# A two-stage conditional residual kernel: first unit of x in three parts, convolution matrices loaded once and copied, the constants' product moved, unit 1 turned in two

## The chip, the cores and the metric

The kernel runs on one core of a Trainium2 chip. The metric is the device time in microseconds of one execution; the median of three runs is given. TensorE (PE) does the matrix products, VectorE (DVE), ScalarE (ACT) and GpSimd (POOL) the elementwise work, and SyncE (SP) and ScalarE each issue DMAs into a queue of their own; 16 DMA engines serve both queues.

## The reference, cut to what matters

Everything is float32. x is 128 samples x 64 channels x 1024 positions.

```python
def L0(x, c, weight, c_weight, bias):      # grouped convolution: 4 groups of 16 channels, 9 taps
    out = conv(x, weight, padding=4, groups=4)
    return out + (c @ c_weight.T)[:, :, None] + bias[None, :, None]

def L1(x, emb, W0, b0, W1, b1, W2, b2, weight, bias_k):
    h = gelu(emb @ W0 + b0); h = gelu(h @ W1 + b1)
    att = softmax(h @ W2 + b2)             # 8 experts for each sample
    agg_w = einsum('bk,koi->boi', att, weight[..., 0])
    agg_b = att @ bias_k
    return einsum('boi,bih->boh', agg_w, x) + agg_b[:, :, None]

x = x + L0(x, cond_128, L0_cond_weight, L0_cond_c_weight, fside_S_0)
x = x + L1(x, cond_128, ...)
```

So each sample gets a grouped convolution, then a 64 x 64 mixing matrix of its own. Both residual sums are folded into the matrices by adding an identity, and everything that does not depend on x is folded into one constant for each sample and output channel.

## The kernel before, in words

**Units.** The 128 samples are worked on in 16 units of 8. Two buffers `xin` and two `xph` are used in turn (the "slot"). For each unit:

1. Eight DMAs bring x into `xin`: halves `i` of the length (0 by SP's queue, 1 by ScalarE's), times `k` in 0, 1 and `t` in 0, 1 (`x_piece`). Partitions hold half, group and sample; each of the 16 partitions of a DMA receives 8 rows of 516 positions.
2. VectorE turns them (`turn_in`, L418) so that 4 neighbouring positions of 16 channels lie on partitions: `xin` to `xph`. The semaphore `turned` counts these turns.
3. TensorE convolves (`conv`, L552): four groups `g`, each 12 matmuls of 64 x 512, with the matrices `wsum` (a view of `wraw`, whose two partition halves hold the same numbers) into a pair of PSUM banks `yps`. Groups take the two pairs in turn, so group `g` waits until VectorE has emptied that of `g-2`.
4. VectorE transposes each group out of PSUM (`y_columns`, L444), and when all four are there it transposes them again into `ynat` (`y_natural`, L453).
5. TensorE mixes (`mix`, L575): four outputs `o` (two samples each), 4 matmuls each, from `ynat` and the unit's mixing matrices `mixv` into `zps`; output `o` waits until `zps` of `o-2` is empty.
6. ScalarE evacuates with the constant added (`evacuate`, L311), two activations an output, and makes `mixv` of the next unit (`matrices`, L320) from the table of all matrices, `mixt`.
7. SP stores each output.

TensorE's order is software-pipelined: conv of unit u, groups 0 and 1; mix of u-1, outputs 0 and 1; conv groups 2 and 3; mix outputs 2 and 3. A matmul is listed as two passes in the trace (float32), so 24 matmuls read x48. Every engine's order is that of its own program (`@block.tensor` and so on); semaphores alone tie them. Units 0 to 2 and the last ones are written out, the others are in loops of two units.

**The opening.** Before the first mix, the small network (`mm`, `act_mlp`, `soft`) gives `att`; GpSimd adds the identities; two aggregates of 16 matmuls each (`aggregate`, L533) produce all mixing matrices, and ScalarE gathers each in two pieces (`gather`, L324). The constants come from one product of `beta` with `consts` (`output_constants`, L651), ScalarE's copy (L359), sums on GpSimd (L275 to L282) and one more product (`pair_constants`, L657). `keep_on` are dummy matmuls on zeros. Unit 0's x comes in two parts and is turned in two (`first_phases`); unit 1's in one part, turned in one.

**ScalarE and SP issue loads in program order**, each load of unit u behind a wait for `turned`, and each instruction after it in the engine's program is behind that wait as well.

## Time and profile before

| | us |
|---|---|
| median of 3 runs | 252.69 |
| lowest, highest | 251.22, 255.4 |
| the profiled execution | 251.88 |
| its span in the profile | 250.1 |

The profiled execution is 1.78 us longer than its span; the difference lies around the span.

| engine | busy us | share of the span |
|---|---|---|
| TensorE | 238.8 | 96% |
| VectorE | 220.8 | 88% |
| ScalarE | 128.5 | 51% |
| GpSimd | 10.4 | 4% |

DMA queue 1 is SP's, queue 10 ScalarE's. In 68.6 MB of traffic the mean is 274 GB/s. Times in a timeline count from the start of the span. A row of it merges neighbouring instructions of one line; its first number is the start, the second the time to the end of the last, and in brackets stands how long the engine was idle before it and what ended that.

### The profile page before, as it was taken

Reading aid. Unit: us, or ns where it says so; the run is one execution under the profiler, and the core shown is the slowest. Engines: PE = TensorE matmul, PEld = TensorE weight load, DVE = VectorE, ACT = ScalarE, POOL = GpSimd, SP = SyncE. Lnnn points to the kernel's source line nnn. Section 1 sums busy time; section 2 is a strip of 40 time slices with the busy share of each in tenths; the row PEclk is TensorE's granted clock in tenths of the full one; section 3 lists DMA queues with packets and bytes.
Section 4 is the critical chain, followed back from the end, with each engine's and each line's share of the span. In section 5 each row is a group of like instructions: output and inputs, shape, how many; then the busy total and the mean of one; then the engine's idle time right before and its main releaser. Section 6 shows DMA issues by size and latency. Waiting matters only on the chain.

```text
span 250.1 us, 5822 instructions
## 1 busy us (share of the span) xinstructions
PE 238.8 (96%) x2186; PEld 103.0 (41%) x2186; DVE 220.8 (88%) x115; ACT 128.5 (51%) x208; POOL 10.4 (4%) x36
## 2 busy tenths in 40 slices
PE   7899899999999999999999999999999999999962
PEld 5633234444343444444443444344443444444631
DVE  0256699999999999999999999999999999999672
ACT  2564106534719083745639181836547286273863
POOL 1323200000000000000000000000000000000000
PEclk9799999999999999999999999999999999999999
DMA  7999935999989999999999998999989895444466
GB/s 201 260 290 273 270 66 184 263 317 369 362 300 303 334 242 375 240 387 233 358 264 313 317 301 310 258 381 229 377 241 348 271 313 242 168 170 169 168 246 260
DMA packets 29771, 68.60 MB, mean 274 GB/s; under 512 B 3312, under 2 KB 5744, under 8 KB 29760
## 3 DMA queue, kind: packets, MB, share of 16 engines
q1 hardware_dynamic: 19824, 51.12, 61.7%
q10 hardware_dynamic: 9936, 17.34, 26.2%
q8 instruction: 7, 0.11, 0.2%
q14 instruction: 4, 0.03, 0.0%
HBM read 34.89 MB, written 33.55 MB: 274 GB/s over the span
## 4 chain that ended last, share of the span: by engine, by line
PE 83%; DVE 5%; DMA 4%; ACT 3%; ACTq 2%; issue 1%
PE yps L552 59%; PE zps L575 21%; DMA xin<-in_x 4%; DVE xph L418 2%; DVE ynat L453 2%; PE yps L591 1%; ACTq L330 1%; PE yps L634 1%; DVE ycol L444 1%; ACT mixv L320 1%; ACT zout L311 1%; DVE ynat L498 1%; PE zps L614 0%; PE yps L614 0%; PE zps L603 0%
## 5 line engine op out<-in xcount | busy, mean ns | idle before, releaser
L552 PE MATMUL yps<-xph,wraw 64*64 64x512 f32 x1488 | 166.7, 589 | 1.7 <-DVE ycol L444 1.1
L552 PEld LDWEIGHTS yps<-xph,wraw 64*64 64x64 f32 x1488 | 66.5, 132 | 95.1 <-issue 95.0
L311 ACT ACTIVATE zout<-zps,gamu 128x512 f32<-128x512 f32 x120 | 72.8, 689 | 29.8 <-PE zps L575 19.9
L444 DVE STREAM_TRANSPOSE ycol<-yps 128x1024 f32<-128x1024 f32 x62 | 74.5, 1227 | 7.3 <-PE yps L552 5.5
L320 ACT ACTIVATE mixv<-mixt 64x256 f32 (+1 forms) x64 | 42.3, 660 | 67.0 <-issue 65.8
L418 DVE STREAM_TRANSPOSE xph<-xin 128x4160 f32<-128x4160 f32 (+2 forms) x17 | 71.8, 4223 | 3.9 <-DMA xin<-in_x 3.9
L453 DVE STREAM_TRANSPOSE ynat<-ycol 128x4096 f32<-128x4096 f32 x15 | 66.7, 4445 | 1.1
L575 PE MATMUL zps<-ynat,mixv 64*64 64x512 f32 x480 | 59.4, 592 | 0.4 <-DVE ynat L453 0.2
L575 PEld LDWEIGHTS zps<-ynat,mixv 64*64 64x64 f32 x480 | 20.6, 132 | 31.6 <-issue 31.2
L250 POOL COPY gamu<-gam 128x4 f32 (+1 forms) x16 | 2.9, 188 | 197.9 <-ACT zout L311 193.2
L634 PE MATMUL yps<-zout 128*128 128x256 f32 x26 | 9.8, 538 | 1.3 <-POOL zout L252 1.3
L634 PEld LDWEIGHTS yps<-zout 128*128 128x128 f32 x26 | 6.7, 271 | 3.3 <-POOL zout L252 1.3
L591 PE MATMUL yps<-xph,wraw 64*64 64x256 f32 x96 | 6.0, 375 | 0.0
L462 DVE TENSOR_REDUCE negmax<-zps 128x1 f32<-128x8 f32 x1 | 0.2, 167 | 6.4 <-PE zps L670 6.4
L491 DVE STREAM_TRANSPOSE ycol<-yps 128x256 f32<-128x256 f32 x8 | 3.1, 424 | 2.6 <-PE yps L591 2.6
L591 PEld LDWEIGHTS yps<-xph,wraw 64*64 64x64 f32 x96 | 4.4, 132 | 2.5 <-issue 1.6
L324 ACT ACTIVATE mixt<-zps 128x1024 f32<-128x1024 f32 x4 | 3.9, 1021 | 2.4 <-PE zps L533 2.4
L498 DVE STREAM_TRANSPOSE ynat<-ycol 128x1024 f32<-128x1024 f32 x4 | 4.7, 1224 | 0.1
L332 ACT ACT_TABLE_LOAD x1 | 1.3, 1283 | 3.8 <-issue 3.8
L603 PE MATMUL zps<-ynat,mixv 64*64 64x512 f32 x16 | 2.2, 600 | 1.0 <-ACT zout L311 1.0
L363 ACT ACTIVATE gam<-zps 128x64 f32<-128x64 f32 x1 | 0.2, 224 | 5.5 <-PE zps L657 5.5
L533 PE MATMUL zps<-zout 32*64 32x512 f32 x32 | 2.9, 612 | 0.0
(54 smaller groups left out, 30.2 us busy)
## 6 DMA issues: line engine op xcount, KB each, us to landing
out<-zout SPq DMA_DIRECT2D x60, 512.0 KB, 4.6
xin<-in_x ACTq DMA_DIRECT2D x60, 258.0 KB, 7.4
xin<-in_x SPq DMA_DIRECT2D x60, 258.0 KB, 7.1
out<-xin SPq DMA_DIRECT2D x2, 512.0 KB, 4.2
out<-xin SPq DMA_DIRECT2D x4, 256.0 KB, 2.8
xin<-in_x ACTq DMA_DIRECT2D x4, 132.0 KB, 5.3
xin<-in_x SPq DMA_DIRECT2D x4, 130.0 KB, 5.9
xin<-in_x SPq DMA_DIRECT2D x4, 128.0 KB, 7.5
```

Of the source, the lines that this page charges most:

```text
L311: nc.scalar.activation(zout[:, o].rearrange("p (i c j q) -> p c i j q", i=2, c=2, q=PH)[:, c], zps[:, at:at + BANK].rearrange("p (q i j) - ...
L320: nc.scalar.activation(mix_places(slot, h, d), mix_values(u, d), ACT.Copy).then_inc(mixv_made, 1)
L324: nc.scalar.activation(mixt[:, a, 2 * RO * i:2 * RO * i + 2 * RO].rearrange("p c b -> p (c b)"), zps[:, 2 * BANK * i:2 * BANK * i + 2 * BA ...
L418: nc.vector.transpose(xph[slot][:, :, :, at:to].rearrange("q g s j t -> q j s g t"), xin[slot][:, :, PH * at:PH * to].rearrange("q c (j p) ...
L444: nc.vector.transpose(ycol[:, :, :, :, :, g].rearrange("p i s j q c -> p (i s j) q c"), yps[:, 2 * BANK * (g % 2):2 * BANK * (g % 2) + 2 * ...
L453: nc.vector.transpose(ynat[slot][:].rearrange("p t q i s (j l) -> p (i s j) q t l", l=16), ycol[:].rearrange("p i s j q g c -> p (i s j q ...
L491: nc.vector.transpose(ycol[:, i, 2 * sh:2 * sh + 2, :, :, g].rearrange("p s j q c -> p (s j) q c"), y_last(g)[:, i].rearrange("p (n j t) - ...
L498: nc.vector.transpose(ynat[1][:, :, :, i, 2 * sh:2 * sh + 2].rearrange("p t q s (j l) -> p (s j) q t l", l=16), ycol[:, i, 2 * sh:2 * sh + ...
L552: last = nc.tensor.matmul(yps[C * c:C * c + C, at:at + BANK].rearrange("p (s f) -> p s f", s=S // 2), wsum[rows, b, g], xph[slot][rows, g, ...
L575: last = nc.tensor.matmul(zps[C * s:C * s + C, at:at + BANK].rearrange("p (n j) -> p n j", j=NJ), mixv[slot][rows, 2 * o + s], ynat[slot][ ...
L591: last = nc.tensor.matmul(y_last(g)[C * c:C * c + C, i].rearrange("p (s f) -> p s f", s=2), wsum[rows, b, g], xph[1][rows, g, 2 * sh:2 * s ...
L634: nc.tensor.matmul(yps[:, 3 * BANK:3 * BANK + BANK // 2], still[:, 0:P], still[:, 0:BANK // 2], start=True, stop=True)
```

## The change

- Unit 0's x comes in three parts instead of two, cut at columns 60 and 95 of 130 (`CUTS`; a column is 4 positions), and is turned in three. A DMA row of 264 to 252 positions becomes rows of 236 or 240, 140, and 140 or 136. ScalarE's 12 x issues of unit 0 are spread between its small steps.
- The convolution matrices, the same on both partition halves, are loaded for 64 partitions; a VectorE copy makes the other 64.
- The mixing weights are issued by ScalarE, not SP; SP issues `consts` ahead of the last part of x.
- An activation on a single column (`spare`) stands right behind the second gelu, so that the exp table's load does.
- The first aggregate goes to `yps` and the second to `zps`, so they no longer wait for each other's gathers; the constants' product goes to a bank of `yps` (`cps`), ahead of the first convolution, with one `keep_on` behind it.
- Unit 1's x is turned in two pieces, before the column transposes of groups 1 and 2 of unit 0.
- `matrices` stands ahead of `load` in ScalarE's program, in the written-out units and in the loop.

```diff
+CUTS = 0, 60, 95, 2 * NJ + 2
+        cps = yps[:, 2 * BANK:3 * BANK]
...
-            sp.dma_start(mixw, mix_w).then_inc(mix_in, 16)
-            for part, there in ((0, x_first), (1, x_in[0])):
+            for part in range(3):
+                if part == 2:
+                    sp.dma_start(consts, const_w).then_inc(const_in, 16)
                 for k in range(KQ):
                     for t in range(2):
-                        sp.dma_start(*x_piece(0, 0, 0, k, t, part)).then_inc(there, 16)
-            sp.dma_start(consts, const_w).then_inc(const_in, 16)
+                        sp.dma_start(*x_piece(0, 0, 0, k, t, part)).then_inc(x_part[part], 16)
...
-                act.wait_ge(turned, u)
+                act.wait_ge(turned, 3 if isinstance(u, int) and u == 2 else u + 2)
...
-            act.dma_start(wraw[:], conv_w).then_inc(w_in, 16)
...
+            def first_load(part, k):
+                for t in range(2):
+                    act.dma_start(*x_piece(0, 0, 1, k, t, part)).then_inc(x_part[part], 16)
+
+            act.dma_start(wraw[0:C], conv_w).then_inc(w_in, 16)
+            act.dma_start(mixw, mix_w).then_inc(mix_in, 16)
+            first_load(0, 0)
+            first_load(0, 1)
...
+            nc.scalar.activation(spare[:], still[:, 0:1], ACT.Exp)
...
+            load_block(1, 1, 0)
+            gather(0, 1, 4)
+            gather(0, 0, 8)
+            act.wait_ge(const_mm, 1)
+            nc.scalar.activation(gprod.rearrange("p e c -> p (e c)"), cps, ACT.Copy).then_inc(const_out, 1)
             load_block(1, 1, 1)
...
                         if o == 1:
+                            matrices(2 * i + c - 3, 1 - c)
                             load(2 * i + c, c)
-                            matrices(2 * i + c - 3, 1 - c)
...
+            def second_phases(c):
+
+                if c == 0:
+                    dve.wait_ge(x_in[1], 128)
+                turn_in(1, (NJ + 2) * c, NJ + 2 + NJ * c)
...
+            dve.wait_ge(w_in, 16)
+            nc.vector.tensor_copy(wraw[C:P], wraw[0:C]).then_inc(w_both, 1)
...
-            first_aggregate()
-            keep_on(3)
-            second_aggregate()
-            pe.wait_ge(w_in, 16)
+            aggregates()
+            output_constants()
+            keep_on(1)
             pe.wait_ge(w_sum, 1)
+
+            pe.wait_ge(agg_out, 2)
             conv(0, 0, 0)
-            conv(0, 0, 1, (output_constants,))
+
+            pe.wait_ge(const_out, 1)
+            conv(0, 0, 1)
```

**ScalarE, units 1 and 2** (L311/L315 evacuates, L294/L298 issues loads of x, L320/L324 makes matrices). Before:

```order
L294 DMA xin<-in_x 16x8x516 x4
L311 ACTIVATE zout<-zps,gamu 128x2x256 x4
L294 DMA xin<-in_x 16x8x516 x4
L320 ACTIVATE mixv<-mixt 64x16x16 x4
L311 ACTIVATE zout<-zps,gamu 128x2x256 x4
```

And changed:

```order
L298 DMA xin<-in_x 16x8x516 x4
L315 ACTIVATE zout<-zps,gamu 128x2x256 x4
L324 ACTIVATE mixv<-mixt 64x16x16 x4
L298 DMA xin<-in_x 16x8x516 x4
L315 ACTIVATE zout<-zps,gamu 128x2x256 x4
```

The four matrices passed ahead of the four issues of the loads; the loop has the same two orders.

**VectorE, from the network's maximum to the natural transpose of unit 0.** Before:

```order
L462 TENSOR_REDUCE negmax<-zps 128x1
L464 RECIPROCAL erec<-esum 128x1
L418 STREAM_TRANSPOSE xph<-xin 128x66x4x4x2
L418 STREAM_TRANSPOSE xph<-xin 128x64x4x4x2
L444 STREAM_TRANSPOSE ycol<-yps 128x128x8
L418 STREAM_TRANSPOSE xph<-xin 128x130x4x4x2
L444 STREAM_TRANSPOSE ycol<-yps 128x128x8 x3
L453 STREAM_TRANSPOSE ynat<-ycol 128x32x4x2x16
```

And changed, from the new copy on:

```order
L475 COPY wraw<-wraw 64x832
L477 TENSOR_REDUCE negmax<-zps 128x1
L479 RECIPROCAL erec<-esum 128x1
L428 STREAM_TRANSPOSE xph<-xin 128x60x4x4x2
L428 STREAM_TRANSPOSE xph<-xin 128x35x4x4x2 x2
L456 STREAM_TRANSPOSE ycol<-yps 128x128x8
L428 STREAM_TRANSPOSE xph<-xin 128x66x4x4x2
L456 STREAM_TRANSPOSE ycol<-yps 128x128x8
L428 STREAM_TRANSPOSE xph<-xin 128x64x4x4x2
L456 STREAM_TRANSPOSE ycol<-yps 128x128x8 x2
L465 STREAM_TRANSPOSE ynat<-ycol 128x32x4x2x16
```

Unit 0's two turns became three, and the one turn of unit 1 (128x130) became two (66 and 64 columns) around the column transpose of group 1.

**TensorE, from the softmax's transpose to the first convolutions.** Before:

```order
L674 MATMUL zps<-shares,att 128x128
L634 MATMUL yps<-zout 128x256 x3
L533 MATMUL zps<-zout 64x512 x8
L634 MATMUL yps<-zout 128x256 x3
L533 MATMUL zps<-zout 64x512 x8
L552 MATMUL yps<-xph,wraw 64x512 x16
L651 MATMUL zps<-zout,beta 128x512
L552 MATMUL yps<-xph,wraw 64x512 x32
```

And changed:

```order
L686 MATMUL zps<-shares,att 128x128
L648 MATMUL yps<-zout 128x256 x3
L547 MATMUL yps<-zout 64x512 x8
L547 MATMUL zps<-zout 64x512 x8
L663 MATMUL yps<-zout,beta 128x512
L648 MATMUL yps<-zout 128x256
L566 MATMUL yps<-xph,wraw 64x512 x48
```

The dummies between the aggregates went, and the constants' product moved from the second group of convolutions to ahead of the first.

## Rows read from the trace of the kernel before

**Rows 1.** The page: busy us (share of the span) xinstructions.

```profile
PE 238.8 (96%) x2186; PEld 103.0 (41%) x2186; DVE 220.8 (88%) x115; ACT 128.5 (51%) x208; POOL 10.4 (4%) x36
```

**Rows 2.** Timeline of TensorE in the loop: start us, us, what.

```profile
38.19 5.37 PE L552 MATMUL yps<-xph,wraw 64*64 64x512 f32 x48
...
51.93 5.37 PE L552 MATMUL yps<-xph,wraw 64*64 64x512 f32 x48
57.09 1.93 PE L575 MATMUL zps<-ynat,mixv 64*64 64x512 f32 x16
58.81 5.37 PE L552 MATMUL yps<-xph,wraw 64*64 64x512 f32 x48
63.97 2.17 PE L575 MATMUL zps<-ynat,mixv 64*64 64x512 f32 x16
65.92 5.37 PE L552 MATMUL yps<-xph,wraw 64*64 64x512 f32 x48
...
225.22 5.37 PE L552 MATMUL yps<-xph,wraw 64*64 64x512 f32 x48
```

**Rows 3.** Timeline of ScalarE in the loop (ACTq is its DMA issuing).

```profile
56.83 2.85 ACTq L294 DMA_DIRECT2D xin<-in_x  x4
59.73 2.72 ACT L320 ACTIVATE mixv<-mixt 64x256 f32<-64x256 f32 x4 [5.92 <-issue]
62.48 2.42 ACT L311 ACTIVATE zout<-zps,gamu 128x512 f32<-128x512 f32 x4
```

**Rows 4.** Timeline of VectorE in the loop, one period apart.

```profile
50.03 2.38 DVE L444 STREAM_TRANSPOSE ycol<-yps 128x1024 f32<-128x1024 f32 x2
...
63.65 2.38 DVE L444 STREAM_TRANSPOSE ycol<-yps 128x1024 f32<-128x1024 f32 x2
```

**Rows 5.** Timeline of VectorE in the opening.

```profile
7.91 0.17 DVE L462 TENSOR_REDUCE negmax<-zps 128x1 f32<-128x8 f32 x1 [6.45 <-PE zps L670]
...
14.86 2.31 DVE L418 STREAM_TRANSPOSE xph<-xin 128x2048 f32<-128x2048 f32 x1 [1.51 <-DMA xin<-in_x]
...
21.91 4.51 DVE L418 STREAM_TRANSPOSE xph<-xin 128x4160 f32<-128x4160 f32 x1 [0.37 <-DMA xin<-in_x]
...
30.57 1.25 DVE L444 STREAM_TRANSPOSE ycol<-yps 128x1024 f32<-128x1024 f32 x1 [1.88 <-PE yps L552]
31.86 4.45 DVE L453 STREAM_TRANSPOSE ynat<-ycol 128x4096 f32<-128x4096 f32 x1
```

**Rows 6.** Timeline of TensorE in the opening.

```profile
12.50 1.11 PE L533 MATMUL zps<-zout 32*64 32x512 f32 x16
...
15.03 1.77 PE L533 MATMUL zps<-zout 32*64 32x512 f32 x16
17.43 3.67 PE L552 MATMUL yps<-xph,wraw 64*64 64x512 f32 x32 [0.62 <-DVE xph L418]
21.02 1.12 PE L651 MATMUL zps<-zout,beta 80*128 80x512 f32 x2
22.08 4.53 PE L552 MATMUL yps<-xph,wraw 64*64 64x512 f32 x40
27.70 2.81 PE L552 MATMUL yps<-xph,wraw 64*64 64x512 f32 x24 [1.09 <-DVE ycol L444]
...
36.45 1.95 PE L575 MATMUL zps<-ynat,mixv 64*64 64x512 f32 x16 [0.25 <-DVE ynat L453]
```

**Rows 7.** Timeline of ScalarE in the opening.

```profile
5.39 1.25 ACTq L339 DMA_DIRECT2D xin<-in_x  x2
```

**Rows 8.** Timeline of GpSimd in the opening.

```profile
15.80 1.27 POOL L270 TENSOR_TENSOR zout<-zout,shares 64x512 f32<-64x512 f32 x1 [4.76 <-DMA zout<-in_const_w]
```

**Rows 9.** DMA traffic of two stretches, 4 to 12 us and 16 to 20 us.

```profile
DMA packets 2314, 2.13 MB, mean 266 GB/s; under 512 B 264, under 2 KB 2299, under 8 KB 2314
...
DMA packets 725, 1.35 MB, mean 337 GB/s; under 512 B 73, under 2 KB 73, under 8 KB 725
```

**Rows 10.** Stretches: us, busy (xcount) PE, PEld, DVE, ACT, POOL; granted clock; DMA share; GB/s.

```profile
6.00:7.00 1.00, 0.29 (x2) 0.09 (x1) 0.00 (x0) 0.31 (x1) 0.00 (x0) 1.00 1.12 294
9.00:10.00 1.00, 1.00 (x4) 0.72 (x3) 0.00 (x0) 0.00 (x0) 0.97 (x4) 0.50 1.11 251
```

More of the change, by code:

```diff
@@ L76, in build @@
         ones = sb("ones", [1, P])
-        warm = sb("warm", [P, 1])
+        warm, spare = sb("warm", [P, 1]), sb("spare", [P, 1])
         negmax, esum, erec = sb("negmax", [P, 1]), sb("esum", [P, 1]), sb("erec", [P, 1])
@@ L145, in build @@
         x_from, x_to = (0, H - PAD), (H + PAD, L)
-        x_cut = [i * H + Q + PAD for i in range(2)]
         def x_piece(slot, u, i, k, t, part=None):
-            at, to = ((x_from[i], x_to[i]) if part is None else
-                      ((x_from[i], x_cut[i]), (x_cut[i], x_to[i]))[part])
+            at, to = x_from[i], x_to[i]
+            if part is not None:
+                at = max(at, H * i + PH * CUTS[part] - PAD)
+                to = min(to, H * i + PH * CUTS[part + 1] - PAD)
             return x_places(slot, i, k, t, at, to - at), x_block(u, k, t, at, to - at)
@@ L193, in load @@
                 if not (isinstance(u, int) and u < 2):
-                    sp.wait_ge(turned, u)
+                    sp.wait_ge(turned, 3 if isinstance(u, int) and u == 2 else u + 2)
                 for k in range(KQ):
@@ L337, in _ @@
             nc.scalar.activation(h1, sps[:, 0:NS], ACT.Gelu, bias=b0s).then_inc(act_mlp, 1)
-            for t in range(2):
-                act.dma_start(*x_piece(0, 0, 1, 1, t, 1)).then_inc(x_in[0], 16)
+            first_load(1, 1)
             act.wait_ge(mm, 2)
             nc.scalar.activation(h2, sps[:, NS:2 * NS], ACT.Gelu, bias=b1s).then_inc(act_mlp, 1)
+            nc.scalar.activation(spare[:], still[:, 0:1], ACT.Exp)
+            first_load(2, 0)
             act.wait_ge(soft, 1)
@@ L365, in _ @@
                 evacuate(0, 0, o)
+                if o == 1:
+                    matrices(1, 1)
                 if o % 2 == 1:
                     load(3 + o // 2, 1 - o // 2)
-                if o == 1:
-                    matrices(1, 1)
             for o in range(PR):
@@ L372, in _ @@
                 if o == 1:
+                    matrices(2, 0)
                     load(5, 1)
-                    matrices(2, 0)
             with act.Fori(3, NU // 2) as i:
@@ L387, in _ @@
             act.wait_ge(gam_cut, NU)
-            act.wait_ge(turned, NU)
+            act.wait_ge(turned, NU + 2)
             def evacuate_first(o, c):
@@ L464, in _ @@
             nc.vector.reciprocal(erec[:], esum[:]).then_inc(soft, 1)
-            first_phases(0)
-            first_phases(1)
+            for part in range(3):
+                first_phases(part)
             y_columns(0, 0)
-            phases(1, 1)
+            second_phases(0)
             y_columns(0, 1)
+            second_phases(1)
             y_columns(0, 2)
@@ L527, in aggregate @@
             def aggregate(a):
-                for r in range(RT):
-                    if a > 0 and r % 2 == 0:
-                        pe.wait_ge(agg_out, 2 * a - 1 + r // 2)
+                for r in ((2, 3, 0, 1), range(RT))[a]:
                     for d in range(2):
-                        nc.tensor.matmul(zps[C * d:C * d + C, BANK * r:BANK * r + BANK],
+                        nc.tensor.matmul((yps, zps)[a][C * d:C * d + C, BANK * r:BANK * r + BANK],
                                          mixw[32 * r:32 * r + 32, 2 * a + d],
@@ L541, in conv @@
                 if g == 0:
-                    pe.wait_ge(turned, u + 2)
+                    pe.wait_ge(turned, 3 if isinstance(u, int) and u == 0 else u + 4)
                 if not (isinstance(u, int) and u < 1 and g < 2):
@@ L649, in output_constants, with pair_constants @@
                 pe.wait_ge(const_eye, 1)
+                pe.wait_ge(agg_out, 1)
+                nc.tensor.matmul(cps, beta[:], consts, start=True, stop=True).then_inc(const_mm, 1)
+            def pair_constants():
                 pe.wait_ge(agg_out, CH)
-                nc.tensor.matmul(gps, beta[:], consts, start=True, stop=True).then_inc(const_mm, 1)
-            def pair_constants():
-                pe.wait_ge(const_out, 1)
                 pe.wait_ge(const_sum, 6)
```

50 lines of the change are left out of this document (19 added, 31 removed).

## The prediction, as it stood before the changed kernel was run

> **What bounds the kernel now.** I read the page's busy shares first: TensorE is busy in 96% of the span and VectorE in 88% [rows 1]. So the span is one stream of matmuls, plus whatever delays its start or breaks it. I then read TensorE's timeline for breaks. After the opening it is regular: 48 convolution passes and 16 mixing passes, start to start 6.88 us (51.93 to 58.81 [rows 2]). From the start at 38.19 to that at 225.22 there are 27 such periods, 187.03 us, where 27 x 6.88 would be 185.6. So about 1.4 us of breaks lie in the loop, and they are not spread evenly: one period of 7.11 us (58.81 to 65.92) is typical of six of them, and each has its excess inside the mixing passes (2.17 us at 63.97 instead of 1.93 at 57.09).
>
> ScalarE's timeline at the same place names the cause [rows 3]. It issues the next unit's four loads in 2.85 us, from 56.83, once VectorE has turned the unit before; only then does it make the mixing matrices (59.73, 2.72 us), and only then evacuate outputs 2 and 3 (62.48 to 64.90). The second mix of TensorE's next pair needs both of those PSUM halves free, and it starts right behind 64.90. ScalarE is half idle and yet late, because its work stands behind an issue that waits. VectorE is the next bound: its own shortest period is 13.62 us [rows 4], against 2 x 6.88 = 13.75 of TensorE.
>
> In the opening, three things end waits [rows 5, 6]. Unit 0's x lands in two parts; VectorE turns the second at 14.86 to 17.17, and the first convolution starts at 17.43, after 0.62 us in which TensorE had nothing to do. Unit 1's x lands at 21.9; it is turned in one piece of 4.51 us, and the column transpose that TensorE needs for group 3 stands behind it, so TensorE idles 1.09 us until 27.70. Then VectorE waits 1.88 us for that group, and starts the natural-order transpose of unit 0 at 31.86; the first mix starts 0.14 us behind its end [rows 6]. From 31.86 both streams run closely packed, so **the time at which this transpose starts (31.86) is what the opening is worth**, one to one.
>
> **The loop.** ScalarE now makes the matrices ahead of the loads. They need only an earlier evacuation and the gathered weights, so they fit in the idle 5.92 us that stands ahead of them now [rows 3]. The loads keep their time, because they wait for the same turned unit in both kernels (the count is raised by two only because units 0 and 1 count two more turns), and four short activations can stand queued while ScalarE's sequencer issues. The evacuation of outputs 2 and 3 follows the issue directly, near 59.8 instead of 62.48, over 2 us before TensorE needs it. **This takes the whole 1.4 us**; VectorE's 13.62 leaves it free, barely. The other end is 0, if some other wait sits in the same place. I take 1.4, since the end of the evacuation and the resumption of the mix coincide.
>
> **The opening on the engines.** ScalarE has one issue more ahead of its first table load (the mixing weights, about 0.4 us). The two matmuls of the small network and its exp shift by about that much; two x issues take 1.25 us [rows 7], and four more of them stand between ScalarE's small steps, each where it waits anyway. The new copy of the convolution matrices on VectorE (64 x 832) is bounded by the 1.25 us column transpose of 1024 elements above [rows 5] and nothing below; it runs in the 6.45 us in which VectorE waits for the network [rows 5], so it costs nothing. Behind it waits only GpSimd's sum on these matrices, which has several us to spare. The aggregates start at 12.50 and 15.03 now, with a gather and dummies between them [rows 6]. Now they stand back to back: twice the 1.11 us of the first, and 0.4 for the delay, end near 15.1. The constants' product needs GpSimd's sum of 1.27 us, which starts at 15.80 today, when its load lands [rows 8]. The load moves ahead of the last x part, so 408 KB less stand before it on SP's queue (mixing weights 128, x 280). At half of 266 GB/s [rows 9] that is 3.1 us: a sum from 13 to 14.3, before TensorE asks. Then the product (1.06, from 21.02 to the next pass at 22.08 in the trace of now) and one dummy of 0.4: TensorE is ready at 16.6, and carries no product between convolutions any more.
>
> **The opening on the DMA queues.** Here the change works against itself. It saves 208 KB of matrices, but x of unit 0, 2048 packets of about 1 KB, becomes 1024 packets of 944 to 960 bytes and 2048 of 544 to 560. The prices: from 4 to 12 us, 2314 packets and 2.13 MB in 8 us, that is 3.46 ns a packet of 920 bytes on average; from 16 to 20 us, 725 packets and 1.35 MB in 4 us, 5.52 ns a packet of 1862 [rows 9]. A straight line through both gives 1.45 ns per packet plus bytes at 457 GB/s. The cut adds 1024 packets and 128 completion packets (16 for each of 8 more DMAs): 1152 x 1.45 ns = +1.7 us. The matrices save 0.21 MB and 64 packets: -0.55 us. Net +1.15 us before unit 1's x is complete. Bounds: by bytes alone the cut is free (net -0.47 us); by packets alone, 1152 x 3.46 ns = +4.0 less 0.2. I take the line, as it uses both rows; 560 bytes lie outside them.
>
> The last part of unit 0 then lands at 14.86 + 1.15 + 0.5 (the constants' load is now ahead of it) less up to 1.2 for traffic of unit 1 that today is served before it and will now be issued after: about 15.7 (13.8 to 17). Its turn is 35 columns of the 64 that take 2.31 us, 1.27 us, so **the first convolution starts near 17.2**, later than TensorE's 16.6. Four groups (twice 5.37), then a column transpose and handovers, 1.4: the natural transpose can start at 17.2 + 12.1 = 29.3.
>
> Unit 1's x lands at 21.9 + 1.15 = 23.0. Two of its eight transfers are now issued by ScalarE behind the constants' copy, near 16 instead of near 11, but the queue ahead of them is hardly empty by then. After it: half a turn 2.38, column 1.2, half a turn 2.31, two columns 2.4: 23.0 + 8.3 = **31.3**. This is the later of the two, so the opening brings 31.86 - 31.3 = 0.55 us. TensorE's 1.09 us stall goes (group 3 needs the column at 26.7), yet VectorE, with unit 1's x, is late next, and takes most of it back.
>
> Sum: 1.4 + 0.55 = 2.0 us off the profiled execution of 251.88 us (span 250.1): 249.9. That execution lies 0.8 below the median of the runs shown, 252.69, whose three values are 4 us apart; I go half of that way and forecast **250.3**.
>
> The Trainium skill, *DMA: Bandwidth & Descriptors*, Specifications, asks for transfers of at least 512 bytes for line rate; pieces of 560 bytes pass, so by it the cut would be free and the sum that of rival A. The rows speak against it: 920-byte packets moved 266 GB/s and 1862-byte ones 337.
>
> **The rivals.**
> (A) *Bytes are all that count.* Unit 1's x lands at 21.9 - 0.5 = 21.4, the last part of unit 0 at 13.8, and TensorE's 16.6 decides the start. The transpose starts at max(16.6 + 12.1, 21.4 + 8.3) = 29.7, or at 28.7 if unit 2's loads press less. Gain 2.2 to 3.2, with the loop 3.6 to 4.6; 251.88 - 4.1 + 0.4 = 248.2. For it: both rows of the line are averages over mixed traffic, and neither measures 560 bytes. Against: the two rates [rows 9]. Chance 0.20. The rule of that page, worked out here, is this case.
> (B) *Packets are all that count*: slower than before. Unit 1's x lands at 21.9 + 3.8 = 25.7, the transpose starts at 34.0, 2.1 late; with the loop's 1.4 the kernel is 0.7 slower: 253.0. It decides as soon as the cut delays unit 1's x by over 3.1 us in all. For it: 560 bytes lie outside both rows, and a fixed cost can rule there. Against: packets of twice the size took 1.6 times as long. Chance 0.10.
> (C) *The loop's breaks stay*, because ScalarE cannot run the matrices beside the issue, or VectorE takes over: only the opening, 251.7. Chance 0.15.
> (D) *The clock.* TensorE was 0.29 busy at 6 to 7 us, and its granted clock was 0.50, the lower of its two levels, at 9 to 10 [rows 10]. A dummy block between aggregates is gone, and about 0.6 us may be idle before the first convolution, or more if x is late. Should some 3 us of the first convolutions run at that level, they would cost 1.6 us more; with a start at 17.2 that gives 30.9, just under the 31.3 of unit 1's x, so it shows only where that x is early or the dip is longer: 250.8. Chance 0.08.
> My forecast, with the opening between -0.3 and +1.3: 0.47.
>
> **How the numbers follow.** The range must reach A and C and most of the scatter of a median; B lies beyond it: 247.7 to 252.6. A measurement here tells about 2% (5 us) from no change. Only the best of A with luck in the runs passes 247.6: 0.08. No case reaches 257.7: 0.02. Within 2%: 0.90.
>
> **What would show it.** Right: all mixing blocks in the loop at 1.93 us; ScalarE's matrices starting before its load issues; the last part of x(0) turned by 17; unit 1's first half turned from 23.0; the natural transpose at 31.3. If the first half turn begins by 21.5, A holds; after 25, B. Mixing blocks of 2.1 us and more mean C; a granted clock of 0.5 past 15 us means D. The forecast is wrong if the natural transpose starts outside 30.5 to 32.2, or if a new wait appears at the constants' product.

## The result, and the profile after

The changed kernel takes **255.75 us** (median of 6 runs, 254.19 to 259.19), the kernel before 252.3 in the same comparison: ratio 1.015, 95% interval 1.0116 to 1.0184. It is slower by 1.5%, where 250.3 was forecast with a range of 247.7 to 252.6; it stays within 2% of the kernel before, as was forecast with 0.90. Ratios leave out the slow runs of a kernel, those more than 1.5% above its fastest, and medians are of all its runs.

The profiled execution took 257.73 us, with a span of 255.9: 5.8 us more than the 250.1 before, and 2 us above its own median, so it shows the loss larger than it mostly is.

The loop first. TensorE's timeline (start us, us, what), answering to [rows 2]:

```profile
52.11 5.37 PE L566 MATMUL yps<-xph,wraw 64*64 64x512 f32 x48
...
58.98 5.37 PE L566 MATMUL yps<-xph,wraw 64*64 64x512 f32 x48
64.14 1.93 PE L589 MATMUL zps<-ynat,mixv 64*64 64x512 f32 x16
65.86 5.37 PE L566 MATMUL yps<-xph,wraw 64*64 64x512 f32 x48
...
231.08 5.37 PE L566 MATMUL yps<-xph,wraw 64*64 64x512 f32 x48
```

and ScalarE's, answering to [rows 3]:

```profile
60.75 2.74 ACT L324 ACTIVATE mixv<-mixt 64x256 f32<-64x256 f32 x4
64.18 2.81 ACTq L298 DMA_DIRECT2D xin<-in_x  x4
67.10 2.42 ACT L315 ACTIVATE zout<-zps,gamu 128x512 f32<-128x512 f32 x4 [3.61 <-PE zps L589]
```

The matrices are made before the issue, and the evacuation starts at 67.10, directly behind the end of the issue (64.18 + 2.81 = 66.99) and about 1 us behind the mix that it empties (64.14 + 1.93); before, it started 3.5 us behind its mix. The profile puts ScalarE's 3.61 us of waiting down to TensorE, but both outputs were computed by 66.07; what it waited for last was its own issue. From 52.11 to 231.08 there are 26 periods of 6.883 us on average, against 6.927 before: the mixing blocks of over 2 us are gone, 1.2 us over the loop. That step did what it was forecast to do.

The opening is where the time went. VectorE, answering to [rows 5]:

```profile
9.56 3.40 DVE L428 STREAM_TRANSPOSE xph<-xin 128x1920 f32<-128x1920 f32 x2
14.75 1.35 DVE L428 STREAM_TRANSPOSE xph<-xin 128x1120 f32<-128x1120 f32 x1 [1.78 <-DMA xin<-in_x]
20.08 1.25 DVE L456 STREAM_TRANSPOSE ycol<-yps 128x1024 f32<-128x1024 f32 x1 [3.98 <-PE yps L566]
29.17 2.38 DVE L428 STREAM_TRANSPOSE xph<-xin 128x2112 f32<-128x2112 f32 x1 [7.84 <-DMA xin<-in_x]
...
37.62 1.25 DVE L456 STREAM_TRANSPOSE ycol<-yps 128x1024 f32<-128x1024 f32 x1 [1.62 <-PE yps L566]
38.91 4.45 DVE L465 STREAM_TRANSPOSE ynat<-ycol 128x4096 f32<-128x4096 f32 x1
```

and TensorE, answering to [rows 6]:

```profile
15.74 1.10 PE L663 MATMUL yps<-zout,beta 80*128 80x512 f32 x2 [0.43 <-ACT mixt L329]
...
17.20 7.97 PE L566 MATMUL yps<-xph,wraw 64*64 64x512 f32 x72
32.82 4.74 PE L566 MATMUL yps<-xph,wraw 64*64 64x512 f32 x24 [7.66 <-DVE ycol L456]
```

The first turn of unit 1's x, which waits for all of it, starts at 29.17 instead of 21.91, 7.26 us later. The two-piece turn gave 2.14 back (group 3 starts at 32.82, 5.12 later than 27.70). Group 3 then took 4.74 us instead of 2.81. The stretches of the same trace (us; busy of PE, PEld, DVE, ACT, POOL; granted clock; DMA share; GB/s) tell why:

```profile
29.00:30.00 1.00, 0.00 (x0) 0.00 (x0) 0.83 (x1) 0.00 (x0) 0.00 (x0) 0.97 1.08 198
33.00:34.00 1.00, 1.00 (x8) 0.40 (x11) 1.00 (x1) 0.00 (x0) 0.00 (x0) 0.50 0.00 0
```

TensorE had idled since 25.2, and its granted clock stood at 0.50, the lower level, from 30 to past 36. So 7.26 - 2.14 + 1.93 = 7.05 us, which is the natural transpose at 38.91 instead of 31.86; less 1.2 of the loop, 5.85, the span's 5.8.

Why was x late? DMA traffic from 14 to 22 us, of before (first group of lines) and of after (second); q1 is SP's queue, q10 ScalarE's; packets, MB, share of 16 engines:

```profile
DMA packets 1326, 2.43 MB, mean 303 GB/s; under 512 B 151, under 2 KB 151, under 8 KB 1326
q1 hardware_dynamic: 735, 1.34, 59.0%
q10 hardware_dynamic: 591, 1.09, 47.0%
```

```profile
DMA packets 1042, 1.92 MB, mean 240 GB/s; under 512 B 112, under 2 KB 112, under 8 KB 1042
q1 hardware_dynamic: 754, 1.39, 79.2%
q10 hardware_dynamic: 288, 0.53, 28.2%
```

The shares of both queues add up to over 100% in either kernel, so the engines had packets at hand. SP's queue moved as much as before, ScalarE's half as much. ScalarE's issues, in the timeline of its queue, and SP's of unit 2 (duration min/median/max in ns, first and last start):

```profile
11.46 0.60 ACTq L298 DMA_DIRECT2D xin<-in_x  x1
12.09 0.62 ACTq L298 DMA_DIRECT2D xin<-in_x  x1
...
16.88 1.39 ACTq L298 DMA_DIRECT2D xin<-in_x  x2
18.37 1.24 ACTq L298 DMA_DIRECT2D xin<-in_x  x2
```

```profile
L202 SPq DMA_DIRECT2D xin<-in_x x4: 577/600/601, 16.1 to 18.0; - x4
```

The first block of unit 1 goes out at 11.46 and the second at 16.88, behind the constants' copy, where the kernel before had 8.1 and 10.9. SP's four of unit 1 go out from 10.23 instead of 8.25, so all eight are later, not two. By 16.88 SP has begun with unit 2.

### The profile page after: what moved, and what is told of

Same layout as the page of the kernel before. It is cut to its first block, busy times and chain, and to the rows that moved or that the text cites. A ratio compares the mean times of both kernels' runs of the same rounds, so it can differ in the third digit from the quotient of the medians.

```text
span 255.9 us, 5835 instructions
## 1 busy us (share of the span) xinstructions
PE 238.2 (93%) x2182; PEld 105.0 (41%) x2182; DVE 220.8 (86%) x118; ACT 127.2 (50%) x209; POOL 10.4 (4%) x36
## 4 chain that ended last, share of the span: by engine, by line
PE 83%; DMA 5%; DVE 4%; ACT 3%; ACTq 2%; issue 1%
PE yps L566 58%; PE zps L589 20%; DMA xin<-in_x 5%; DVE ynat L465 2%; PE yps L648 2%; ACTq L334 2%; PE yps L605 1%; DVE ycol L456 1%; DVE xph L428 1%; ACT mixv L324 1%; ACT zout L315 1%; DVE ynat L514 0%; PE yps L547 0%; PE zps L628 0%; PE yps L663 0%
## 5 line engine op out<-in xcount | busy, mean ns | idle before, releaser
L566 PE MATMUL yps<-xph,wraw 64*64 64x512 f32 x1488 | 168.4, 595 | 7.7 <-DVE ycol L456 7.7
L315 ACT ACTIVATE zout<-zps,gamu 128x512 f32<-128x512 f32 x120 | 72.8, 689 | 95.7 <-PE zps L589 76.3
L566 PEld LDWEIGHTS yps<-xph,wraw 64*64 64x64 f32 x1488 | 67.8, 134 | 100.9 <-issue 100.8
L428 DVE STREAM_TRANSPOSE xph<-xin 128x4160 f32<-128x4160 f32 (+4 forms) x19 | 72.0, 3795 | 9.8 <-DMA xin<-in_x 9.8
L589 PE MATMUL zps<-ynat,mixv 64*64 64x512 f32 x480 | 58.3, 589 | 0.3 <-DVE ynat L465 0.3
L324 ACT ACTIVATE mixv<-mixt 64x256 f32 (+1 forms) x64 | 42.4, 663 | 1.9 <-ACT mixt L329 0.7
L589 PEld LDWEIGHTS zps<-ynat,mixv 64*64 64x64 f32 x480 | 21.9, 133 | 29.1 <-issue 28.7
L648 PE MATMUL yps<-zout 128*128 128x256 f32 x22 | 8.7, 552 | 1.3 <-POOL zout L256 1.3
L648 PEld LDWEIGHTS yps<-zout 128*128 128x128 f32 x22 | 5.8, 279 | 2.8 <-POOL zout L256 1.3
L605 PEld LDWEIGHTS yps<-xph,wraw 64*64 64x64 f32 x96 | 4.4, 132 | 2.5 <-issue 1.6
L475 DVE COPY wraw<-wraw 64x832 f32<-64x832 f32 x1 | 0.6, 586 | 3.3 <-DMA wraw<-in_conv_w 3.3
L617 PE MATMUL zps<-ynat,mixv 64*64 64x512 f32 x16 | 2.2, 600 | 1.0 <-ACT zout L315 1.0
L329 ACT ACTIVATE mixt<-yps 128x1024 f32<-128x1024 f32 x2 | 1.9, 1020 | 2.1 <-PE yps L547 2.1
```

What stands on the lines that cost most here:

```text
L315: nc.scalar.activation(zout[:, o].rearrange("p (i c j q) -> p c i j q", i=2, c=2, q=PH)[:, c], zps[:, at:at + BANK].rearrange("p (q i j) - ...
L324: nc.scalar.activation(mix_places(slot, h, d), mix_values(u, d), ACT.Copy).then_inc(mixv_made, 1)
L428: nc.vector.transpose(xph[slot][:, :, :, at:to].rearrange("q g s j t -> q j s g t"), xin[slot][:, :, PH * at:PH * to].rearrange("q c (j p) ...
L566: last = nc.tensor.matmul(yps[C * c:C * c + C, at:at + BANK].rearrange("p (s f) -> p s f", s=S // 2), wsum[rows, b, g], xph[slot][rows, g, ...
L589: last = nc.tensor.matmul(zps[C * s:C * s + C, at:at + BANK].rearrange("p (n j) -> p n j", j=NJ), mixv[slot][rows, 2 * o + s], ynat[slot][ ...
L605: last = nc.tensor.matmul(y_last(g)[C * c:C * c + C, i].rearrange("p (s f) -> p s f", s=2), wsum[rows, b, g], xph[1][rows, g, 2 * sh:2 * s ...
```

## Experiments

**1. The late block, three ways.** Theory L: the late issue alone. *issue_early*, on the changed kernel:

```diff
             load_block(1, 1, 0)
+            load_block(1, 1, 1)
             gather(0, 1, 4)
...
-            load_block(1, 1, 1)
             gather(1, 0, 12)
```

> The changed kernel, with ScalarE's second block of unit 1's x (two transfers of 258 KB) issued right behind its first block again, ahead of the gathers, near 12.7 to 14 us instead of 16.9 to 18.3. Theory L (late issue: the block stands behind the constants' copy and so falls behind unit 2's loads on the DMA engines): unit 1's x is complete by 21 to 22.5 instead of 29.2, TensorE's 7.7 us of waiting for group 3 goes, the natural transpose of unit 0 starts at 29.5 to 31 instead of 38.9, and the kernel takes 247.5 to 250 where the one before takes 252.3. Rival P (the smaller packets and more transfers of unit 0 are what delays unit 1's x): the block's place changes little, unit 1's x still lands after 26, time 253 to 255.5. Rival S (unit 2's loads, which SP issues 1.1 us earlier than in the kernel before, take the engines in any case): lands at 24 to 26, time 250.5 to 252.5.

Measured: 254.06 us (251.6 to 255.69), ratio 1.006 (1.0033 to 1.0087), 0.9% better than the changed kernel's 1.015. Unit 1's x still came late (in the slowest of the twelve runs, 255.69):

```profile
27.98 2.38 DVE L428 STREAM_TRANSPOSE xph<-xin 128x2112 f32<-128x2112 f32 x1 [5.43 <-DMA xin<-in_x]
```

Theory L in this simple form fell: issuing at 12.4 to 15.0 does not do. P's numbers (after 26, 253 to 255.5) were met, so this run alone does not refute P; *late_on_before* and *cut_only* below do. What the trace shows instead is a queue alone. From 16 to 18 us SP's had the engines to itself, at under 200 GB/s:

```profile
DMA packets 221, 0.39 MB, mean 197 GB/s; under 512 B 30, under 2 KB 30, under 8 KB 221
q1 hardware_dynamic: 221, 0.39, 107.2%
```

*sp_hold*, on the changed kernel:

```diff
-                    sp.wait_ge(turned, 3 if isinstance(u, int) and u == 2 else u + 2)
+                    sp.wait_ge(turned, 4 if isinstance(u, int) and u == 2 else u + 2)
```

> The changed kernel, with SP's loads of unit 2 held until the first half of unit 1 has been turned (count 4 instead of 3); ScalarE's late second block of unit 1 stays at 16.9. Theory L with unit 2 as the competitor: without SP's traffic after 16 us the two late transfers have the engines almost alone, land 4 to 6 us after their issue, so unit 1's x is complete at 22 to 24, and the kernel takes 249.5 to 251.5. Rival P: lands at 27 or later, time above 254. Rival Q (one queue alone gets only the 200 to 220 GB/s that the trace shows where the other is idle, and is slow whoever competes): lands at 24 to 26, time 251.5 to 253.5.

Measured: 253.84 us, ratio 1.0088 (1.0066 to 1.0111), 0.6% better than the changed kernel:

```profile
25.78 2.38 DVE L428 STREAM_TRANSPOSE xph<-xin 128x2112 f32<-128x2112 f32 x1 [4.66 <-DMA xin<-in_x]
```

The landing is in rival Q's range, the time 0.3 us above it. Without unit 2's traffic 3.4 of the 7.26 us go and the rest stays. ScalarE's queue, alone from 24 to 28 us, moved 199 GB/s, so the late queue is slow when nothing competes too.

*late_on_before*, on the kernel before:

```diff
-            load_block(1, 1, 1)
             gather(0, 0)
...
             gather(1, 1)
+            load_block(1, 1, 1)
```

> The kernel before, with one edit: ScalarE's second block of unit 1's x issued behind the four gathers, near 17 us instead of 10.9. Theory L: the loss appears without any other part of the change; unit 1's x lands at 26 to 29 instead of 21.9, the natural transpose of unit 0 starts 4 to 7 us later, time 256.5 to 259.5. Rival P: the kernel before keeps its larger pieces, so it loses under 1.5 us, time 252.3 to 254. Rival S: within 1 us as well.

Measured: 255.67, 261.28, 262.11 and 262.46 us, too few and too far apart for a ratio. Even the lowest is 3.8 us above the median of the kernel before (251.83), without any other part of the change. P and S, which allowed up to 254 and up to 1 us, are out. L's range began at 256.5; why the other three runs lose about 10 us is open. In the run of 261.28:

```profile
30.05 4.51 DVE L418 STREAM_TRANSPOSE xph<-xin 128x4160 f32<-128x4160 f32 x1 [6.89 <-DMA xin<-in_x]
```

**2. The matrices ahead of the loads, alone.** *swap_on_before*: `matrices` ahead of `load` at the three places, as in the change.

> The kernel before, with the mixing matrices ahead of the loads in ScalarE's program and nothing else. My step on the loop: the six long mixing blocks go, 1.4 us less, ratio 0.993 to 0.996, time 250.6 to 251.3. Rival: they depend on how the two streams happen to lie after the opening and come back elsewhere, ratio 0.999 to 1.001.

Measured: 250.57 us, ratio 0.9954 (0.9934 to 0.9974), 1.3 us below the kernel before (251.83 in that comparison). Every full mixing block of its loop takes 1.92 or 1.93 us, so the step on the loop is shown by itself.

**3. Which part of the pairing counts.** Theory H now: each half of the partitions takes some 200 GB/s, SP fills one and ScalarE the other, and whoever issues late leaves a half idle. *halves_mixed*, on the changed kernel (SP likewise, `x_piece(slot, u, i, 0, t)`):

```diff
-            def load_block(u, slot, k):
-                for t in range(2):
-                    act.dma_start(*x_piece(slot, u, 1, k, t)).then_inc(x_in[slot], 16)
+            def load_block(u, slot, t):
+                for i in (1, 0):
+                    act.dma_start(*x_piece(slot, u, i, 1, t)).then_inc(x_in[slot], 16)
```

> The changed kernel, with the eight transfers of a unit (units 1 to 15) dealt out otherwise: SP issues k=0 of both halves of the length by turns, ScalarE k=1 of both by turns; before, SP wrote only partitions 0 to 63 and ScalarE only 64 to 127. Places and times of issue stay. Theory H (the two queues are served in about the order of issue, so after a late issue one queue runs alone, and alone it moves 200 GB/s because it writes one half of the partitions; both halves together take 335 to 340): the stretches at 200 GB/s between 14 and 30 us go up to 300 or more, unit 1's x is complete at 22 to 25 instead of 29.2, time 249.5 to 252. Rival R (a queue alone gets 200 GB/s whatever it writes): rates stay, lands at 28 to 30, time 253.5 to 256. The Trainium skill, SBUF - State Buffer, section Door 1, says that DMA bandwidth depends on how many of 16 ports the partitions reach, and partitions 64 and up use the other eight; by it H.

Measured: 258.82 us, ratio 1.0272 (1.0222 to 1.0322), unit 1's turn at 31.00: worse than both theory H (249.5 to 252) and rival R (253.5 to 256). The rates stayed, as R says: 204 to 245 GB/s in every 2 us from 14 to 30. The same edit on *swap_on_before*, *mixed_on_swap*:

> The kernel before with the matrices ahead of the loads, and the transfers of units 1 to 15 dealt out so that each queue writes both halves of the partitions by turns. Theory H: the stretches with one queue alone (12 to 14, 20 to 24, 28 to 32 us at 195 to 235 GB/s) get faster, unit 1's x lands up to 1 us earlier than 21.7, time 249.5 to 250.5; the loop gains nothing, its loads land 10 us ahead of need. Rival R: no change from the swap alone, 250.6. It can lose, landing at 22 to 24, if both queues now often write the same half at once.

Measured: 253.73 us, ratio 1.0052 (1.0016 to 1.0087), 1% above the swap alone in ratio (0.9954), unit 1's turn at 23.31. Here both queues work side by side from 16 to 20 us, and yet:

```profile
DMA packets 582, 1.07 MB, mean 267 GB/s; under 512 B 65, under 2 KB 65, under 8 KB 582
```

where the kernel before moved 337 in the same stretch [rows 9]. My expectation that a lone queue would speed up was wrong. It fits that its transfers are worked through one after the other, each in one half, and that two busy queues whose halves sometimes coincide lose; neither run shows which half a packet went to.

*port_bench* tests the halves by themselves, with loads behind the last store of the kernel before:

> The kernel before, with four stretches of loads after its last store, one after the other (the results are not touched; the time is longer by them and not compared): (1) SP alone, 8 transfers of 258 KB into partitions 0 to 63; (2) SP alone, 4 transfers of 512 KB into all 128 partitions; (3) SP into partitions 0 to 63 and ScalarE into 64 to 127, 4 transfers each at the same time; (4) both queues into 0 to 63. If the halves set the rate: about 200, 300 or more, 335, 200 GB/s. If the number of queues sets it: 200, 200, 335, 335. If the size of a row does: (2) alone rises, (1) and (3) alike.

DMA traffic inside the four stretches, in their order:

```profile
DMA packets 865, 1.59 MB, mean 199 GB/s; under 512 B 95, under 2 KB 95, under 8 KB 865
...
DMA packets 439, 1.61 MB, mean 402 GB/s; under 512 B 46, under 2 KB 46, under 8 KB 439
...
DMA packets 955, 1.78 MB, mean 254 GB/s; under 512 B 95, under 2 KB 95, under 8 KB 955
q1 hardware_dynamic: 488, 0.91, 53.3%
q10 hardware_dynamic: 467, 0.87, 52.2%
...
DMA packets 753, 1.39 MB, mean 199 GB/s; under 512 B 78, under 2 KB 78, under 8 KB 753
q1 hardware_dynamic: 399, 0.74, 56.7%
q10 hardware_dynamic: 354, 0.66, 50.6%
```

One queue into partitions 0 to 63: 199 GB/s. One queue into all 128: 402 (its rows are of 4 KB, not 2, and one transfer covers all partitions, not 16). Two queues into the same half: 199 again. So the number of queues does not set the 200; where they write does. That it is the half is not separated from the narrower reading: in the fourth stretch both queues issue their transfers for the same 16 partitions in the same order, and no run sent 4 KB rows into one half. Two queues into both halves, started together, gave 254 and not 335. The rate per us shows them taking turns: from 274 to 275 us SP's queue moved 97 packets and ScalarE's 26, in the next 22 and 104, at 231 GB/s both times. The Trainium skill, SBUF - State Buffer, section Door 1, has DMA bandwidth depend on how many of 16 ports the partitions reach, eight of them for partitions 0 to 63; by that, the trace agrees (199 and 402).

*paired_issue*, on the changed kernel:

```diff
             first_load(2, 1)
+            load_block(1, 1, 0)
             act.wait_ge(share_in, 16)
...
-            load_block(1, 1, 0)
+            load_block(1, 1, 1)
             gather(0, 1, 4)
...
-            load_block(1, 1, 1)
             gather(1, 0, 12)
```

> The changed kernel, with ScalarE's two blocks of unit 1's x where the kernel before has them: the first ahead of the four scaled attention copies (near 10.5), the second right behind these (near 12), so that they stand beside SP's four at 10.2 to 12.9. Theory H: both halves are written at the same time, 330 GB/s from 14.5 on, unit 1's x complete at 20.5 to 22; TensorE waits under 1 us for group 3; natural transpose of unit 0 at 29 to 30.5; time 248 to 249.5, under both kernels. Rival P (small packets): lands after 24, time over 251. If only lateness counted and not the pairing, this would equal the run with both blocks behind the copies (254.1).

Measured: 250.57 us (248.9 to 253.16), ratio 0.9956 (0.9918 to 0.9994): 1.9% (5 us) less than the changed kernel by moving four issues, two by about 1 us and two by 5. Above the 248 to 249.5 expected, but with all other parts of the change in place. In its profile, the fastest run:

```profile
22.44 2.38 DVE L428 STREAM_TRANSPOSE xph<-xin 128x2112 f32<-128x2112 f32 x1 [1.34 <-DMA xin<-in_x]
...
30.44 4.45 DVE L465 STREAM_TRANSPOSE ynat<-ycol 128x4096 f32<-128x4096 f32 x1
```

The 330 GB/s that I expected from 14.5 us on came only from 19 us on. From 14 to 18 both queues worked, each into its own half, and moved little more than one alone:

```profile
DMA packets 489, 0.90 MB, mean 226 GB/s; under 512 B 51, under 2 KB 51, under 8 KB 489
q10 hardware_dynamic: 262, 0.50, 59.0%
q1 hardware_dynamic: 227, 0.40, 48.8%
```

So pairing the issues makes the high rate possible and does not ensure it. What it does bring here is that ScalarE's transfers are no longer served behind SP's of unit 2.

*sp_takes_block*: ScalarE's late `load_block(1, 1, 1)` goes, and in SP's program

```diff
             load(1, 1)
+            for t in range(2):
+                sp.dma_start(*x_piece(1, 1, 1, 1, t)).then_inc(x_in[1], 16)
             load(2, 0)
```

> The changed kernel, with the two late transfers of unit 1's x (258 KB each, partitions 96 to 127) issued by SP right behind its own four, near 12.9 to 14.1 us, and no longer by ScalarE at 16.9. Theory O (the queues are served in about the order of issue, whatever queue it is; the loss comes from two transfers issued behind unit 2's): unit 1's x complete at 21.5 to 24, time 249.5 to 252.5. Rival (it is ScalarE's queue that is slow, in itself): no difference to see between this and an early issue by ScalarE, whose run took 251.6 to 255.7. If the smaller pieces were the cause, it stays at 255.

Measured: 253.19 us, ratio 1.0056 (0.9999 to 1.0113), unit 1's turn at 24.51, both just outside theory O's ranges. The landing is 3.5 us before that of *issue_early*, but the time is the same (ratio 1.006), which is what the rival had said; the run decides nothing by its time. That ScalarE's queue is not slow in itself rests on the rates of a queue alone: SP's 197 GB/s (*issue_early*, 16 to 18 us), ScalarE's 199 (*sp_hold*, 24 to 28).

**4. The other parts.** *two_turns*, on *swap_on_before*: `second_phases` as in the change, and the counts of `turned`.

> The kernel before with the matrices ahead of the loads and unit 1 turned in two pieces around the column transpose of group 1; x, weights and product as before. My formula: the natural transpose of unit 0 starts at the landing of unit 1's x (21.7) + 8.3 = 30.0 instead of 31.7, TensorE's 1.06 us wait goes, so 1.5 us less than the run with the swap alone (250.6): 249.1, ratio to before 0.987 to 0.991. Rival: the column that group 3 needs is only 2.2 us earlier while the natural transpose waits for the same end of the convolutions, gain under 0.5 us.

Measured: 248.92 us (248.33 to 249.36), ratio 0.9886 (0.9849 to 0.9922), 1.65 below the swap alone:

```profile
22.27 2.38 DVE L418 STREAM_TRANSPOSE xph<-xin 128x2112 f32<-128x2112 f32 x1 [0.23 <-DMA xin<-in_x]
...
31.04 4.45 DVE L457 STREAM_TRANSPOSE ynat<-ycol 128x4096 f32<-128x4096 f32 x1
```

That is 8.77 us from landing to natural transpose, where I had 8.3: in 0.58 of it VectorE waits for group 3.

*both_before*, on *two_turns*: `load_block(1, 1, 1)` directly behind `load_block(1, 1, 0)`, ahead of the attention copies.

> The run with two turns (248.92), with both of ScalarE's blocks of unit 1's x issued ahead of the attention copies, 8.5 to 11 us, beside SP's four at 8.3 to 10.9. If pairing the issue times is what keeps both halves of the partitions busy, unit 1's x is complete at 20.8 to 21.7 instead of 22.2 and the natural transpose of unit 0 starts 0.3 to 0.7 us earlier, 248.3 to 248.7. Rival: already paired enough, under 0.2 us, or the attention copies, now up to 0.5 us later, take it back.

Measured: 248.53 us, ratio 0.9858 (0.9827 to 0.9888); natural transpose at 30.36. That is 0.4 us less than *two_turns*, as expected, but the intervals overlap: a gain is not shown.

*old_loads*, on *paired_issue*:

```diff
-CUTS = 0, 60, 95, 2 * NJ + 2
+CUTS = 0, NJ + 2, 2 * NJ + 2
...
-            act.dma_start(wraw[0:C], conv_w).then_inc(w_in, 16)
-            act.dma_start(mixw, mix_w).then_inc(mix_in, 16)
+            act.dma_start(wraw[:], conv_w).then_inc(w_in, 16)
```

(`mixw` is issued by SP again, and the copy goes.)

> The run with the paired issue (250.57 median, 248.9 to 253.2), with the opening's loads as in the kernel before: unit 0's x in two parts, the convolution matrices loaded whole and not copied, mixing weights from SP; the constants' load ahead of the last part, the product ahead of the convolutions and unit 1 in two turns stay. If the three parts, the half load and the copy are what separates the paired run from the run with two turns alone (248.92), this gives 248.3 to 249.3, and little scatter. If it is the product and the aggregates' new place, it gives 250 to 251.5. The constants' load has 1 KB pieces ahead of it, so the product may wait 1 us.

Measured: **248.17 us** (248.03 to 248.97), ratio 0.985 (0.9818 to 0.9881): the fastest of all here. TensorE convolves all four groups in one stretch and VectorE does not wait for x:

```profile
18.24 10.54 PE L561 MATMUL yps<-xph,wraw 64*64 64x512 f32 x96
```

```profile
15.24 2.31 DVE L426 STREAM_TRANSPOSE xph<-xin 128x2048 f32<-128x2048 f32 x1 [1.24 <-DMA xin<-in_x]
...
22.30 2.34 DVE L426 STREAM_TRANSPOSE xph<-xin 128x2112 f32<-128x2112 f32 x1
```

*cut_only* and *half_weights* put back the three parts, or the half load with its copy and the mixing weights issued by ScalarE:

> The run old_loads (248.17: product ahead, unit 1 in two turns, matrices ahead of loads, transfers paired), with unit 0's x in three parts at 60 and 95 again, ScalarE's issues spread as in the changed kernel; weights whole, mixing weights by SP. If the three parts cost the 2.4 us (twelve issues instead of eight put ScalarE's transfers of unit 1's x two issues later, 10.5 to 13.2, so less paired with SP): 249.5 to 251, with scatter. If they cost nothing: 248 to 248.6. If my packet price (+1.7 us) were right, the landing of unit 0's last part would move to 16 or later; bytes alone leave it near 14.9.

> The run old_loads, with the convolution matrices loaded for 64 partitions and copied by VectorE, and the mixing weights issued by ScalarE; x in two parts. 208 KB less to load, at 200 to 340 GB/s 0.6 to 1 us, so unit 0's x lands that much earlier: 247.4 to 248.1. Rival: ScalarE's extra issue shifts its x transfers by 0.6 us against SP's and costs as much, 248.2 to 249.5.

Measured: 249.45 us, ratio 0.9923 (0.9896 to 0.9951), and 248.9, ratio 0.9885 (0.9853 to 0.9917). The three parts cost about 0.7% in ratio; of the half load no gain can be seen, where 247.4 to 248.1 was expected. *cut_only* also tests the packet price by itself. With it the last part of unit 0 would be turned from 16 or later. It was turned from 15.12, against 15.24 in *old_loads*:

```profile
15.12 1.35 DVE L428 STREAM_TRANSPOSE xph<-xin 128x1120 f32<-128x1120 f32 x1 [1.68 <-DMA xin<-in_x]
```

So the 1024 packets more did not delay it.

*late_on_old_loads*, on *old_loads*: ScalarE's two blocks of unit 1 where the changed kernel has them.

> The run old_loads, with ScalarE's first block of unit 1's x behind the attention copies and the second behind the constants' copy, as in the changed kernel; all other loads as in the kernel before. If the late issue is the whole cause of the loss, it takes 253.5 to 257 and unit 1's x lands at 26 to 30. If the loss needs the new parts as well, under 251.

Measured: ten runs from 250.48 to 257.83 us, median 255.3. Five of them, 250.48 to 253.75, give the ratio 1.0003 (0.996 to 1.0046), 1.5% or about 3.8 us above *old_loads*; the other five, 256.85 to 257.83, lie about 9 us above it, and why the times scatter so is open. In the profiled one (257.32), unit 1's x was turned from 28.47, in the range expected, and ScalarE's transfers issued at 12.49 and 13.11 got nothing from 14 to 18 us while SP's, issued from 8.35, were served:

```profile
DMA packets 440, 0.80 MB, mean 199 GB/s; under 512 B 48, under 2 KB 61, under 8 KB 440
q1 hardware_dynamic: 440, 0.80, 107.7%
```

So the loss appears without the new loads of the change.

*best*, on *old_loads*: both blocks ahead of the attention copies.

> The run old_loads, with both of ScalarE's blocks of unit 1's x ahead of the attention copies (near 8.9 to 11.4), as in both_before, which took 0.4 us off two_turns. Expected 247.7 to 248.1; the same as old_loads (248.17) if VectorE already starts the turn of unit 1 without waiting, as its trace shows (22.30 straight behind the column transpose).

Measured: 249.07 us (248.23 to 250.98), ratio 0.9902 (0.9867 to 0.9938): no gain over *old_loads*, where 247.7 to 248.1 was expected; in its profile, of 250.71 us, the last part of unit 0 was turned at 16.09 to 18.40 instead of 15.24, and TensorE waited 1.79 us. *old_loads* stays the one to take.

## Why the prediction was wrong, point by point

- **The loop: right.** 1.4 us were forecast for the matrices ahead of the loads, 1.3 measured alone, 1.2 in the profile. (27 x 6.88 is 185.8 and not 185.6, so the rows too gave 1.3.) Rival C, that the breaks stay, is out.
- **The engines in the opening: right in kind and nearly in size.** The copy took 0.59 us and hid; GpSimd's sum started at 12.27; the exp came 0.7 us later and not 0.4 (9.10 against 8.37); the first convolution started at 17.20, forecast near 17.2. That the number fits is luck: x was turned by 16.1, and the product with its dummy, from 15.74, set the start, behind a wait of 0.43 us for ScalarE's gather. A new wait at that product was one of the prediction's signs of being wrong. It cost nothing here, because group 3 waited for unit 1's x far longer. One reading contradicts its own numbers: with convolutions from 17.2, TensorE asks for group 3's column at 25.2, so a column at 26.7 does not end the stall but makes it about 1.5 us. In *paired_issue* the stall is 1.16. The sum does not hang on it.
- **The packet price: wrong, and on the wrong side.** I took 1.45 ns a packet, hence unit 0's last part at 15.7. It was there at 14.75, halfway to the 13.8 of bytes alone, so the landing does not decide; *cut_only* against *old_loads* does (15.12 and 15.24). From 8 to 10 us the changed kernel moved 925 packets, 0.48 MB, at 242 GB/s, which is what 1 KB pieces got before (246). Rows 9 do not show what a packet costs. In the trace of before alone, packets of 2 KB moved at 195 GB/s from 30 to 32 us and at 339 from 18 to 20; the row that I took is among the highest. Nor was the slower row one of a queue alone, since from 4 to 12 us both were equally busy:

```profile
q1 hardware_dynamic: 1175, 1.05, 56.8%
q10 hardware_dynamic: 1139, 1.08, 55.5%
```

Why those 1 KB pieces moved at a mean of only 266 GB/s stays open. The Trainium skill's limit of 512 bytes (DMA: Bandwidth & Descriptors, section Specifications), which I had set aside, agrees in that the 560 byte pieces moved no slower than the 1 KB ones; neither came near the 337 GB/s of the 2 KB row.
- **The step that failed: "Two of its eight transfers are now issued by ScalarE behind the constants' copy, near 16 instead of near 11, but the queue ahead of them is hardly empty by then."** I asked only whether that queue ran dry, and priced the move at nothing; nor did I see that ScalarE's other two transfers moved too, from 8.1 to 11.5. From 14 to 16 us SP's queue had 102% and ScalarE's 7%, from 20 to 22 SP's 110% and ScalarE's 0.2%, and from 28 to 30 ScalarE's was alone (107%), at 198 to 231 GB/s each time. Unit 1's x landed at 29.2, forecast 23.0. The late second block alone, on the kernel before, loses 3.8 us in the lowest of its four runs, both late blocks on *old_loads* 1.5% (3.8 us) in the lower half of theirs, while undoing both on the changed kernel wins 1.9% (5 us): shown from both sides. Of the 7.26 us, 3.4 go when unit 2's traffic, now served in between, is held back (*sp_hold*). That a queue alone moves 200 because it writes one half of the partitions rests on *port_bench*, with the gap named there.
- **The rivals.** A had the packets right and missed the late x. B named the right sign and place (unit 1's x after 25) with a cause that is refuted. D's price was named for another idle stretch; the clock did fall, to 0.50, but behind a wait of 7.7 us, and cost 1.9. No rival looked at the two queues as a pair, though the trace of before shows both rates (337 GB/s from 16 to 20 us, 195 from 30 to 32 with SP's queue all but alone).
- **The two turns: right in kind, undersized.** They brought 1.65 us alone, where 0.55 us was all that the sum left for the whole opening; 0.55 rested on the packet price.

Open: by what rule the engines choose between the queues. The order of issue fits the traces here, but no run varied it alone. Open too is what lets two queues in two halves move 337 GB/s in one stretch and 226 or 254 in another, why the late kernels' times scatter by 7 us, and why *cut_only* loses 0.7%: its later issues or its pieces.

## What to carry to other kernels

Transfers that together make one operand should be issued side by side by both queues, each into another half of the partitions; when a kernel moves one issue behind a wait, ask also what its partner will be served first, and how fast a queue alone is (here 200 GB/s against up to 340 for the pair). Before fitting a price per packet, look for stretches with packets of one size at different rates: where there are any, the line through two rows measures something else. And look for work of an engine that stands behind its own waiting DMA issue: moving that work ahead took 1.3 us out of a loop at no cost.

## What the runs showed of the hardware

- Loads of 2 KB rows into partitions 0 to 63 moved at 199 GB/s, from one queue or from two; one queue with 4 KB rows into all 128 partitions reached 402 (*port_bench*). Two queues, one half each, moved from 226 (*paired_issue*, 14 to 18 us) to 337 GB/s (the kernel before, 16 to 20).
- A queue whose transfers were issued 4.1 us after the first of the other's got nothing for 4 us (*late_on_old_loads*, 14 to 18 us), and the times of that kernel scatter from 250.48 to 257.83.
- Pieces of 560 bytes moved as fast as pieces of 1 KB: 242 against 246 GB/s in the same stretch of the opening.
- TensorE had no matmul for 7.66 us; its granted clock fell to 0.50 in that time and was still there for the first 3.9 us of work: 24 passes in 4.74 us instead of 2.81.
